# Degrees by a search in the sorted targets; all edge chunks scored behind the node projection

## Chip, cores and metric

The kernel runs on one core of one Trainium2 chip. The metric is the device time of one execution in microseconds (us): the median of three runs before was 3279.69 us (3274.05 to 3285.43). Engines: PE is TensorE (PEld its weight loads), DVE is VectorE, ACT is ScalarE, POOL is GpSimd, SP is SyncE; SPq and POOLq are the queues on which SyncE and GpSimd issue transfers.

## The reference, cut to what matters

Two rounds of a graph layer and a mixture-of-experts layer over N = 6250 nodes of D = 256 features and E = 100000 edges; `dst` is sorted. The change lies in the first stage of the first graph layer, on normed node rows:

```python
ft = (feat @ W_fc).reshape(N, H, D)               # H = 8 heads of 32
eh = jnp.einsum('nhd,hd->nh', ft, attn_h)
et = jnp.einsum('nhd,hd->nh', ft, attn_t)
fe = (edge_attr @ W_e).reshape(-1, H, D)          # 64 numbers an edge
ee = jnp.einsum('ehd,hd->eh', fe, attn_e)
e = leaky_relu(eh[src] + ee + et[dst])
... # softmax of e over the edges of each dst, then the weighted sum of ft[src]
```

Later stages also need the in-degree of every node (a mean over its edges) and the rank of every node among those that have edges.

## The kernel before

The program is a row of phases: `front` (L282 to L840), `attend` (L843 on: softmax and sums of the first graph layer), the gated experts, `sum_segments`, `mean_route` and `expert_tiles`. A phase ends with a barrier of all engines. Every order of work in `front` is written out by hand, one in-order list for each engine, with semaphores between them. `front` has these strands:

- **Node projection.** 50 columns of 125 nodes, two columns a group, so NGR = 25 groups. SyncE loads x in ten pieces (`load_x`, L400). VectorE takes statistics (`stats`, L694) and norms two columns (`norm`, L711). TensorE turns them (`turn`, L544: 4 transposes) and multiplies by the weights, extended by attn_h and attn_t (`project`, L553: 8 matmuls into two PSUM banks of which there is one set, so group g+1 waits until ScalarE has emptied group g). ScalarE copies the turned tile (`copy_turned`, L635) and empties the banks (`rows`, L641), whose two row buffers SyncE stores to the DRAM table `ft_rows` (`store`, L415). `rows(g)` waits for the store of group g-2.
- **Edge scores.** 49 chunks of 16 x 128 edges (NCH = 49), half a megabyte each, in four load buffers (`load`, L404: it waits until the chunk four before it is turned). TensorE turns a chunk (`turn_edges`, L517: 8 transposes), ScalarE copies it (`copy_edges`, L616), TensorE multiplies it by the folded edge weights (`score`, L528: 16 matmuls), ScalarE keeps the scores in the tile V (`keep`, L624). Chunks 0 to 24 run inside the 25 projection groups, chunks 25 to 48 behind them. `keep(0)` waits until the zeroes for `et_at_starts`, which SyncE stores from V, have landed (L442).
- **Degrees.** VectorE splits every dst into two digits (L722 to L728) and writes one-hots of both for each of the 49 chunks (`onehots`, L685), two chunks a group; TensorE counts them by 784 small matmuls into one bank (`count`, L537). Behind the last group VectorE turns the counts into degrees, prefix sums, first edges (FIRSTI) and ranks (L772 to L798).
- **GpSimd.** When the table of et is stored, it gathers one tile (L497), then scatters et to the first edge of each node by 50 indirect transfers (L503), which need FIRSTI, then gathers the first 64 of attend's 784 tiles of `ft_rows` (L511). The phase ends when all strands have ended. In attend GpSimd gathers the other 720 tiles (L975).
- **Ranks of edges.** VectorE marks where an edge has the dst of the one before it (CONTB, CONT) and scans these to ranks (L801 to L809). SyncE stores and reloads them in other layouts through DRAM, one transfer waiting for another (L454 to L476); the last of these is CONTU, a 1568 KB load that repeats its source eight times. No edge chunk is loaded while SyncE works through this list from L463 to L476. TensorE turns the ranks at one place among the chunks (`late`, L602 to L611).
- **The end.** SyncE loads the scattered et back into F (L481) once the scatters have landed, three chunks ahead of the last load. VectorE fills the gaps by 8 scans (L835), adds F to V in 7 parts (L840), and SyncE stores each part (L488) for attend.

Of the kernel before, what the change touches and what calls it, by code (L numbers as in the profile page):

```python
# [18 lines left out]
bf16 = mybir.dt.bfloat16  # L19
i32 = mybir.dt.int32  # L20
# [5 lines left out]
P = 125  # L26
# [255 lines left out]
def front(nc, sb, ps, sem, sems, x, src, dst, edge_attr, W_fc, attn_h, attn_t, W_e, attn_e, GX, a_in, ident, iota, below,  # L282
# [20 lines left out]
    with ExitStack() as s:  # L303
# [3 lines left out]
        ZB = sb(s, "ZB", [128, 128], bf16)  # L307
# [12 lines left out]
        HS = 4  # L320
        FB = F[:, :].bitcast(bf16)
        hotA = [FB[:, k * C * P:(k + 1) * C * P].rearrange("p (c a) -> p c a", a=P) for k in range(HS)]
        hotB = [FB[:, HS * C * P + k * C * NT:HS * C * P + (k + 1) * C * NT].rearrange("p (c b) -> p c b", b=NT)
                for k in range(HS)]
        QI = sb(s, "QI", [QB, NQ, EP], i32)
        QF = sb(s, "QF", [QB, NQ, EP])
        DA = sb(s, "DA", [EP, ES])
# [10 lines left out]
        DT = XNB[0:NT, NQ * EP:NQ * EP + P]  # L338
        CONTQ = QI[:, :, :].bitcast(bf16)[:, :, 0:EP]
        INC = sb(s, "INC", [P, 2, NT])  # L340
        NEQ = sb(s, "NEQ", [P, NT])
        UN = sb(s, "UN", [P, NT])
        TOT = sb(s, "TOT", [P, 2])
# [8 lines left out]
        BASEF = DA[0:1, :]  # L352
# [12 lines left out]
        w_ready, vb_ready, zb_ready = sem("w_ext_ready"), sem("vb_ready"), sem("zb_ready")  # L365
# [5 lines left out]
        hot, hot_used, counted = sem("hot"), sem("hot_used"), sem("degrees_counted")  # L371
        dt_ready, deg_ready, tot, pre, first_ready = (sem("degrees_copied"), sem("degrees_T"), sem("node_totals"),
                                                      sem("node_prefix"), sem("firsts_ready"))
# [14 lines left out]
        with nc.Block() as block:  # L388
            @block.sync
            def _(sp):  # L390
# [80 lines left out]
                sp.wait_ge(dt_ready, 1)  # L471
# [44 lines left out]
            def _(pe):  # L516
# [2079 lines left out]
```

## Time and profile before

| What | us |
|---|---|
| median of 3 runs | 3279.69 |
| the profiled execution: its own time / its span | 3277.21 / 3275.7 |
| front, up to the first instruction of attend | 401.2 |
| PE, DVE, POOL busy in the span | 2385.6, 1885.0, 1795.3 |

The trace is one execution. A window row gives its stretch and length, then the busy time (and number of instructions) of PE, PEld, DVE, ACT and POOL, then the granted TensorE clock as a share of full speed, the busy share of the 16 DMA engines, and GB/s. A timeline row gives start, duration, engine, line, operation, the tile written and read, the number of instructions merged, and in brackets the idle time before and what ended it; a row of merged ones shows their common stretch. A grouped line gives the number of instructions, their busy time and mean ns, and the idle time before them.

### The profile page before, as it was taken

The page shows a single profiled execution, that of the slowest core. Times are in us where ns is not written, and L with a number is a line of the kernel's source. Part 1 is how long each engine was busy: PE and PEld are TensorE (multiplying, and loading weights), DVE is VectorE, ACT ScalarE, POOL GpSimd, SP SyncE. Part 2 cuts the span into 40 slices and gives each one's busy share as a digit, 9 for nine tenths or more (in the row PEclk, how much of TensorE's full clock was granted, in tenths as well). Part 3 has the DMA queues.
Part 4 walks back from the last instruction along what each step waited for, and adds up shares of the span by engine and source line. Part 5 has one row for each costly group of instructions (what it writes and reads, how often), then busy time and mean ns, then how long its engine had stood idle before and what let it go on. Part 6 is the DMA issues. An engine that isn't in the chain of part 4 may idle for free. (4 is left out here: it accounts for less than half of the span.)

```text
span 3275.7 us, 49346 instructions
## 1 busy us (share of the span) xinstructions
PE 2385.6 (73%) x12682; PEld 1986.9 (61%) x12682; DVE 1885.0 (58%) x5767; ACT 1315.9 (40%) x4659; POOL 1795.3 (55%) x1886
## 2 busy tenths in 40 slices
PE   5995366667666665657899698888888888746088
PEld 4884256666666565446677576666666666635077
DVE  7981388888889887657455433333333333366245
ACT  2332255555555544523445333333333333355033
POOL 0007777777777777041000677777777777250645
PEclk9998778887888877778999656656565566757589
DMA  7336644444444445460000333333333333321342
GB/s 209 100 109 149 201 110 112 113 112 112 112 111 114 112 112 153 139 185 26 23 16 19 113 106 105 107 105 106 105 106 105 106 105 106 113 62 34 97 139 86
DMA packets 264113, 348.42 MB, mean 106 GB/s; under 512 B 153632, under 2 KB 193686, under 8 KB 262331
## 3 DMA queue, kind: packets, MB, share of 16 engines
q0 software_dynamic: 87936, 235.05, 25.3%
q1 hardware_dynamic: 175908, 110.32, 13.1%
q8 instruction: 103, 1.69, 0.2%
q14 instruction: 166, 1.36, 0.1%
HBM read 288.25 MB, written 61.20 MB: 107 GB/s over the span
## 5 line engine op out<-in xcount | busy, mean ns | idle before, releaser
L1384 POOL DMA_INDIRECT Gb<-normed_rows,SRCT x784 | 741.3, 946 | 519.6 <-SPq L1376 281.0
L1405 PE MATMUL pAb<-HOTb,Gb 128*128 128x128 f32 x3136 | 845.5, 426 | 149.4 <-DMA Gb<-normed_rows,SRCT 117.5
L1405 PEld LDWEIGHTS pAb<-HOTb,Gb 128*128 128x128 f32 x3136 | 659.6, 297 | 335.4 <-DMA Gb<-normed_rows,SRCT 274.7
L1445 DVE TENSOR_TENSOR ACC<-ACC,pAb 128x256 f32 x784 | 330.8, 422 | 641.8 <-PE pAb L1405 569.1
L975 POOL DMA_INDIRECT GX<-ft_rows,SRCT x432 | 413.3, 957 | 131.8 <-issue 128.6
L1064 ACT ACTIVATE ACC<-apA 128x254 f32 x784 | 300.4, 383 | 413.5 <-PE apA L1137 339.4
L1137 PE MATMUL apA<-AHOT,GX 128*128 128x129 f32 x1920 | 306.2, 330 | 81.1 <-DVE GX L1286 80.8
L1137 PEld LDWEIGHTS apA<-AHOT,GX 128*128 128x128 f32 x1920 | 292.2, 243 | 98.8 <-DVE GX L1286 98.6
L1424 ACT ACTIVATE HOTb<-OFFb 128x1024 f32<-128x1024 f32 x98 | 103.6, 1057 | 604.8 <-PE pAb L1405 604.7
L975 POOL DMA_INDIRECT G<-ft_rows,SRCT x288 | 273.8, 951 | 87.6 <-issue 87.1
L1420 ACT ACTIVATE OFFb<-iota,NRELb 128x128 f32<-128x128 f32 x784 | 239.6, 388 | 6.7
L1137 PE MATMUL apA<-AHOT,G 128*128 128x129 f32 x1216 | 192.3, 327 | 52.1 <-DVE G L1286 50.0
L1137 PEld LDWEIGHTS apA<-AHOT,G 128*128 128x128 f32 x1216 | 182.2, 239 | 64.4 <-DVE G L1286 62.1
L1286 DVE TENSOR_TENSOR GX<-GX,apV 128x1024 f32<-128x1024 f32 x120 | 143.1, 1193 | 0.0
L1614 POOL DMA_INDIRECT Y<-sums_by_rank,RANKI x50 | 48.4, 967 | 170.0 <-POOLq L152 80.8
L1065 ACT ACTIVATE FL<-apA 128x4 f32<-128x4 f32 x784 | 135.0, 172 | 0.0
L533 PE MATMUL pS<-VB,eT 128*128 128x128 f32 x784 | 105.2, 290 | 39.9 <-ACT V L628 22.8
L497 POOL DMA_INDIRECT C<-et_rows,DXI x1 | 2.6, 2577 | 233.7 <-DMA et_rows<-ETS 233.7
L533 PEld LDWEIGHTS pS<-VB,eT 128*128 128x128 f32 x784 | 96.3, 201 | 47.8 <-ACT eT L622 46.1
L2454 POOL DMA_INDIRECT out_dram<-sO,sID x80 | 77.8, 972 | 77.6 <-issue 40.9
L1186 DVE TENSOR_TENSOR AHOT<-apL,RELT 128x1024 f32<-128x1024 f32 x98 | 118.7, 1211 | 0.0
L1941 PE MATMUL fpM<-fxT,ffn_E 128*128 128x250 f32 x400 | 100.3, 405 | 25.0 <-ACT h L1869 25.0
(381 smaller groups left out, 4182.4 us busy)
## 6 DMA issues: line engine op xcount, KB each, us to landing
ebuf<-in_edge_attr_dram SPq DMA_DIRECT2D x49, 448.0 KB
Gb<-normed_rows,SRCT POOLq DMA_INDIRECT x784, 2.7
rows_by_expert<-ffn_PADT SPq DMA_DIRECT2D x1, 10360.0 KB, 42.3
sT<-rows_by_expert SPq DMA_DIRECT2D x80, 129.5 KB, 2.1
GX<-ft_rows,SRCT POOLq DMA_INDIRECT x480
sums_by_rank<-rrowa SPq DMA_DIRECT2D x49, 128.0 KB, 1.7
sums_by_rank<-rrowb SPq DMA_DIRECT2D x49, 128.0 KB, 1.7
GX<-in_x_dram SPq DMA_DIRECT2D x11, 560.0 KB
```

Of the source, the lines that this page charges most:

```text
L533: last = nc.tensor.matmul(pS[:, m * 2 * H0:m * 2 * H0 + 128], eT[c % 2][:, m * EP:(m + 1) * EP], VB[:, :], start=True, stop=True)
L975: pool.indirect_dma_start(G[c % GS][:, m, :], None, FT[:, :], bass.IndirectOffsetOnAxis(ap=SRCT[:, t:t + 1], axis=0)).then_inc(g_in[c % GS ...
L1064: nc.scalar.activation(acc[:, :, ds(r + 1, EP - 1)], sums[:, :, 1:EP], ACT.Copy)
L1065: nc.scalar.activation(FL[:, :, f:n + 1:n - f], sums[:, :, 0:HW:EP], ACT.Copy).then_inc(pfree[b], 1)
L1137: last = nc.tensor.matmul(pA[b][:, f * HW:(f + 1) * HW], G[c % GS][:, m, f * 128:(f + 1) * 128], HOT[c % 2][:, m, :], start=True, stop=True)
L1186: nc.vector.tensor_tensor(HOT[c % 2][:, h * HT:(h + 1) * HT, 0:EP], pL[0:EP, 256:256 + EP].unsqueeze(1).to_broadcast([EP, HT, EP]), RELT[: ...
L1286: nc.vector.tensor_tensor(v, v, pV[0:EP, 0:128].rearrange("p (h m) -> p h m", m=UT)[:, :, m:m + WB].rearrange("p h m -> p m h").unsqueeze( ...
L1384: pool.indirect_dma_start(G[g % R][m][:, :], None, TABLE[:, :], bass.IndirectOffsetOnAxis(ap=SRCT[:, t:t + 1], axis=0)).then_inc(g_in[g % ...
L1405: last = nc.tensor.matmul(pA[b][:, o:o + EP], G[k][m][:, c * 128:(c + 1) * 128], HOT[k % 2][:, m, :], start=True, stop=True)
L1420: nc.scalar.activation(OFF[k2][:, m, :], iota[0:EP, 0:EP], ACT.Abs, bias=NREL[k2][:, m:m + 1])
L1424: nc.scalar.activation(HOT[k2][:, :, :], OFF[k2][:, :, :], ACT.Relu, bias=1.0, scale=-1.0).then_inc(hot[k2], 1)
L1445: last = nc.vector.tensor_tensor(acc[:, :, ds(b, EP)], acc[:, :, ds(b, EP)], pA[q][:, o:o + KD * EP].rearrange("p (c r) -> p c r", c=KD), ...
```

## The change

- The digits, `onehots` and `count` go, with their zero matmuls and the transpose of the counts. In place of them: SyncE loads dst once more in another layout (DVI: 125 partitions of 25 x 32 sorted targets; SNI: the first target of the next partition). GpSimd makes two tables of node numbers. VectorE makes, in four batches of 12 or 13 columns, a one-hot of the partition that holds each node's first edge (`segment_hits`, 13 x 125 numbers in each of two instructions); TensorE fetches that partition's 25 word starts by 51 matmuls (`segments`, at groups 1 to 4); VectorE counts those below the node (`segment_rows`) and so knows the 32-word row. GpSimd gathers these rows by NV = 51 indirect transfers, ahead of everything it did before; VectorE counts inside them (`first_edges`) and gets first edges and, by differences, degrees. FIRSTI no longer needs the prefix matmul on TensorE.
- All 49 chunks are turned and scored behind the projection. Inside the projection SyncE issues no edge load beyond the first four.
- The small matmuls for ranks sit at chunks 12 and 13, the turn of ranks at chunk 24. The SyncE list of rank transfers begins behind the load of chunk 16.
- F is loaded behind the last edge load (it waits for `rq_ready` too, since F's memory now also holds BASEF), instead of three chunks ahead of it.

```diff
+        NV = NT + 1
+        SB = 13
+        SW = [min(SB, NV - b * SB) for b in range((NV + SB - 1) // SB)]
+        BW = 32
+        BK = E // BW // P
+        HITS = SB * P
+        NODE = F[0:P, 0:HITS]
+        OH = [F[0:P, (1 + k) * HITS:(2 + k) * HITS] for k in range(2)]
+        WORDS = F[:, HITS:HITS + NV * BW].bitcast(i32)
+        WORDF = F[0:P, HITS + NV * BW:HITS + 2 * NV * BW]
+        LT = F[0:P, 3 * HITS:3 * HITS + SB * BK]
+        DVI = F[0:P, 3 * HITS + SB * BK:3 * HITS + SB * BK + BK * BW].bitcast(i32)
...
+                ds32 = dst.rearrange("(p j) -> p j", j=BK * BW)
+                for a in PARTS:
+                    sp.dma_start(DVI[a, :], ds32[a, :]).then_inc(dv_in, 16)
+                sp.dma_start(SNI[0:P - 1, :], ds32[1:P, 0:1], allow_slow_non_contiguous=True).then_inc(dv_in, 16)
...
                 for g in range(NGR):
-                    if g > 0:
-                        load(g - 1 + ER)
                     store(g)
                 sp.dma_start(ETD.rearrange("(p i) h -> p (i h)", i=NT), ETS[0:P, :]).then_inc(etd_out, 16)
-                n = NGR - 1 + ER
-                load(n)
+                n = 4 * ER
+                for c in range(ER, n + 1):
+                    load(c)
...
-                for c in range(n + 3, NCH - 3):
+                for c in range(n + 3, NCH):
                     load(c)
+                sp.wait_ge(rq_ready, 1)
                 sp.wait_ge(st, 16 * NT)
                 sp.dma_start(F[:, :], STARTD.rearrange("(p j) h -> p (j h)", j=ES)).then_inc(f_in, 16)
-                for c in range(NCH - 3, NCH):
-                    load(c)
...
+                pool.wait_ge(rows_ready, 1)
+                dw = dst.rearrange("(r k) -> r k", k=BW)
+                for i in range(NV):
+                    pool.indirect_dma_start(WORDS[:, i * BW:(i + 1) * BW], None, dw,
+                                            bass.IndirectOffsetOnAxis(ap=ROWI[:, i:i + 1], axis=0)).then_inc(words_in, 16)
...
-                def count(c):
-                    pe.wait_ge(hot, c + 1)
-                    for m in range(C):
-                        last = nc.tensor.matmul(pH[0:NT, 0:P], hotB[c % HS][:, m, :], hotA[c % HS][:, m, :],
-                                                start=False, stop=False, skip_group_check=True)
-                    last.then_inc(hot_used, 1)
+                def segments(b):
+                    pe.wait_ge(oh_ready, b + 1)
+                    if b:
+                        pe.wait_ge(seg_read, b)
+                    for i in range(SW[b]):
+                        o = i * (BK + 1)
+                        last = nc.tensor.matmul(pH[0:P, o:o + 128], OH[b % 2][:, i * P:(i + 1) * P], SEG[:, :], start=True, stop=True)
+                    last.then_inc(seg_found, 1)
...
-                    turn_edges(g)
-                    count(2 * g)
+                    if 1 <= g <= len(SW):
+                        segments(g - 1)
                     if g + 1 < NGR:
                         turn(g + 1)
-                    if 2 * g + 1 < NCH:
-                        count(2 * g + 1)
-                    score(g)
                     project(g)
-                nc.tensor.matmul(pH[0:NT, 0:P], ZB[:, 0:NT], ZB[:, 0:P], start=False, stop=True,
-                                 skip_group_check=True).then_inc(counted, 1)
-                turn_edges(NGR)
-                pe.wait_ge(dt_ready, 1)
-                nc.tensor.transpose(pQ[0:P, 0:NT], DT[:, :], ident[0:NT, 0:NT]).then_inc(deg_ready, 1)
-                score(NGR)
-                turn_edges(NGR + 1)
-                pe.wait_ge(tot, 1)
-                for n in range(2):
-                    last = nc.tensor.matmul(pQ[0:P, 64 + n:65 + n], below[0:P, 0:P], TOT[:, n:n + 1], start=True, stop=True)
-                last.then_inc(pre, 1)
-                score(NGR + 1)
-                pe.wait_ge(rtot, 1)
-                nc.tensor.matmul(pT[:, 0:1], below[:, :], TOTR[:, :], start=True, stop=True).then_inc(rpre, 1)
...
-                    copy_edges(g)
                     if g + 1 < NGR:
                         copy_turned(g + 1)
-                    keep(g)
                     rows(g)
                     if g + 3 < NGR and chunk_of(g + 3) > chunk_of(g + 2):
                         root(chunk_of(g + 3))
-                copy_edges(NGR)
-                for c in range(NGR, NCH):
+                copy_edges(0)
+                for c in range(NCH):
...
+                def segment_hits(b):
+                    if b >= 2:
+                        dve.wait_ge(seg_found, b - 1)
+                    w = SW[b] * P
+                    nc.vector.tensor_scalar(OH[b % 2][:, 0:w], NODE[:, 0:w], SNX[:, b:b + 1], None, ALU.is_le)
+                    dve.drain()
+                    nc.vector.scalar_tensor_tensor(OH[b % 2][:, 0:w], NODE[:, 0:w], SX[:, b:b + 1], OH[b % 2][:, 0:w], ALU.is_gt,
+                                                   ALU.mult).then_inc(oh_ready, 1)
...
+                    v = pH[0:P, 0:w * (BK + 1)].rearrange("p (i k) -> p i k", k=BK + 1)
+                    lt = LT[:, 0:w * BK].rearrange("p (i k) -> p i k", k=BK)
+                    nc.vector.tensor_tensor(lt, v[:, :, 0:BK], NODEV[:, a].unsqueeze(2).to_broadcast([P, w, BK]), ALU.is_lt)
+                    nc.vector.tensor_copy(ROWF[:, a], v[:, :, BK]).then_inc(seg_read, 1)
+                    dve.drain()
+                    nc.vector.tensor_reduce(LESS[:, a], lt, AX.X, ALU.add)
...
+                def first_edges():
+                    dve.wait_ge(words_in, 16 * NV)
+                    nc.vector.tensor_copy(WORDF, WORDS[0:P, :])
+                    dve.drain()
+                    v = WORDF.rearrange("p (i k) -> p i k", k=BW)
+                    nc.vector.tensor_tensor(v, v, NODEV[:, :].unsqueeze(2).to_broadcast([P, NV, BW]), ALU.is_lt)
+                    dve.drain()
+                    nc.vector.tensor_reduce(LESS[:, :], v, AX.X, ALU.add)
+                    dve.drain()
+                    nc.vector.scalar_tensor_tensor(ROWF[:, :], ROWF[:, :], float(BW), LESS[:, :], ALU.mult, ALU.add)
+                    dve.drain()
+                    nc.vector.tensor_tensor(DEG[:, :], ROWF[:, 1:NV], ROWF[:, 0:NT], ALU.subtract)
...
-                    for c in range(2 * g + 2, min(2 * g + 4, NCH)):
-                        onehots(c)
+                    if 1 <= g <= len(SW):
+                        segment_rows(g - 1)
+                        if g + 1 < len(SW):
+                            segment_hits(g + 1)
...
+                nc.vector.tensor_tensor(FIRSTI[0:P, :], ROWF[:, 0:NT], UN[:, :], ALU.add).then_inc(first_ready, 1)
+                dve.wait_ge(f_ready, NGR)
+                nc.vector.tensor_tensor(CONT[:, :], DX[:, 1:ES + 1], DX[:, 0:ES], ALU.is_equal)
                 dve.wait_ge(pre, 1)
```

## Rows read from the trace of the kernel before

**Rows 1.** Busy time by stretch: the projection, the edge stage, the start.

```profile
54.00:234.00 180.00, 170.96 (x1547) 149.40 (x1546) 158.26 (x218) 62.04 (x191) 0.00 (x0) 0.98 0.37 104
295.00:360.00 65.00, 48.09 (x398) 44.15 (x397) 24.09 (x25) 20.09 (x48) 50.38 (x49) 1.00 0.79 230
16.00:56.00 40.00, 21.01 (x153) 18.37 (x154) 38.42 (x64) 5.54 (x18) 0.00 (x0) 0.87 0.99 293
```

**Rows 2.** Busy time in a stretch of attend; grouped lines of GpSimd in attend.

```profile
600.00:800.00 200.00, 137.80 (x837) 124.77 (x836) 176.23 (x611) 106.34 (x554) 151.56 (x160) 0.83 0.46 112
L975 POOL DMA_INDIRECT GX<-ft_rows,SRCT x432 | 413.3, 957 | 131.8 <-issue 128.6 <-PE apA L1137 3.3
```

**Rows 3.** Timeline of GpSimd: start us, duration us, what (later timelines alike).

```profile
244.79 1.21 POOL L503 DMA_INDIRECT et_at_starts<-ETS,FIRSTI  x1 [0.31 <-issue]
308.88 1.00 POOL L511 DMA_INDIRECT GX<-ft_rows,SRCT  x1 [0.30 <-issue]
393.99 0.94 POOL L511 DMA_INDIRECT G<-ft_rows,SRCT  x1 [0.30 <-issue]
401.17 0.10 POOL L935 MEMSET HSEL<- 128x8 f32 x1 [6.25 <-POOLq L152]
```

**Rows 4.** Timeline of TensorE, chunks 25, 47 and 48.

```profile
234.99 1.09 PE L524 MATMUL pE<-ident,ebuf 128*128 128x128 f32 x8
353.32 1.04 PE L524 MATMUL pE<-ident,ebuf 128*128 128x128 f32 x8
357.28 1.04 PE L524 MATMUL pE<-ident,ebuf 128*128 128x128 f32 x8
359.38 2.02 PE L533 MATMUL pS<-VB,eT 128*128 128x128 f32 x16 [1.06 <-ACT V L628]
```

**Rows 5.** Timeline of SyncE and VectorE at the front's end.

```profile
331.57 0.35 SPq L481 DMA_DIRECT2D F<-et_at_starts  x1
345.36 14.05 DVE L835 TENSOR_TENSOR_SCAN F<-xnT,C,F 128x784 f32<-128x784 f32 x8 [30.10 <-DMA F<-et_at_starts]
359.49 7.12 DVE L840 TENSOR_TENSOR V<-V,F 128x896 f32<-128x896 f32 x7
360.60 6.91 SPq L488 DMA_DIRECT2D score_parts<-V  x7
```

**Rows 6.** Timeline of SyncE and TensorE around the longest wait.

```profile
245.16 0.34 SPq L458 DMA_DIRECT2D edge_rank<-DB  x1
260.96 0.65 SPq L476 DMA_DIRECT2D CONTU<-goes_on_by_tile  x1
261.66 0.45 SPq L408 DMA_DIRECT2D ebuf<-in_edge_attr_dram  x1
284.77 1.97 PE L524 MATMUL pE<-ident,ebuf 128*128 128x128 f32 x8 [24.66 <-DMA ebuf<-in_edge_attr_dram]
291.24 1.92 PE L524 MATMUL pE<-ident,ebuf 128*128 128x128 f32 x8
```

**Rows 7.** Timeline of one projection group, TensorE and SyncE.

```profile
139.76 2.00 PE L560 MATMUL pF<-Wext,xnT 128*125 128x272 f32 x8
143.59 0.65 PE L549 MATMUL pT<-ident,xn 125*128 125x125 f32 x4
142.63 0.76 SPq L418 DMA_DIRECT2D ft_rows<-row  x2
```

**Rows 8.** Timeline of ScalarE and TensorE, first groups.

```profile
46.87 0.28 ACT L628 ACTIVATE V<-pS 128x128 f32<-128x128 f32 x1 [12.35 <-DMA sums_by_rank<-V]
52.46 3.06 PE L560 MATMUL pF<-Wext,xnT 128*125 128x272 f32 x8
```

**Rows 9.** Grouped lines of VectorE in the projection.

```profile
L689 DVE TENSOR_TENSOR F<-iota,DA 128x2000 bf16<-128x2000 f32 x41 | 91.6, 2235 | 0.0
L716 DVE TENSOR_SCALAR xn<-GX,MEAN,RSTD 125x256 f32<-125x256 f32 x40 | 14.7, 409 | 0.6
L279 DVE BATCH_NORM_STATS2 ST<-GX 125x6 f32<-125x256 f32 x40 | 13.8, 413 | 0.0
```

More of the change, by code:

```diff
@@ L318, in front @@
         eT = [sb(s, f"eT{k}", [128, C // 2 * EP]) for k in range(2)]
[L320 to L324, printed above, removed]
+        NV = NT + 1
[10 more added lines that the diff above has]
+        DVI = F[0:P, 3 * HITS + SB * BK:3 * HITS + SB * BK + BK * BW].bitcast(i32)
+        SNI = sb(s, "SNI", [P, 1], i32)
+        SX = sb(s, "SX", [P, len(SW)])
+        SNX = sb(s, "SNX", [P, len(SW)])
+        SEG = sb(s, "SEG", [P, 128])
+        NODEV = sb(s, "NODEV", [P, NV])
+        ROWF = sb(s, "ROWF", [P, NV])
+        LESS = sb(s, "LESS", [P, NV])
+        ROWI = sb(s, "ROWI", [128, NV], i32)
         QI = sb(s, "QI", [QB, NQ, EP], i32)
         QF = sb(s, "QF", [QB, NQ, EP])
-        DA = sb(s, "DA", [EP, ES])
         DB = sb(s, "DB", [EP, ES])
@@ L370, in front @@
         sc_ready, v_ready = sem("edge_scores"), sem("edge_scores_kept")
-        hot, hot_used, counted = sem("hot"), sem("hot_used"), sem("degrees_counted")
-        dt_ready, deg_ready, tot, pre, first_ready = (sem("degrees_copied"), sem("degrees_T"), sem("node_totals"),
-                                                      sem("node_prefix"), sem("firsts_ready"))
+        dv_in, node_set = sem("dst_segments_in"), sem("node_numbers_set")
+        oh_ready, seg_found, seg_read = sem("segment_onehots"), sem("segments_found"), sem("segments_read")
+        rows_ready, words_in = sem("dst_rows_known"), sem.gather("dst_rows_in")[0]
+        tot, pre, first_ready = sem("node_totals"), sem("node_prefix"), sem("firsts_ready")
         etd_out, cont_ready, cont_out, cq_in = sem("et_out"), sem("cont_ready"), sem("cont_out"), sem("cont_by_tile")
@@ L562, in project @@
                     last.then_inc(f_ready, 1)
-                pe.wait_ge(zb_ready, 1)
-                nc.tensor.matmul(pH[0:NT, 0:P], ZB[:, 0:NT], ZB[:, 0:P], start=True, stop=False, skip_group_check=True)
                 pe.wait_ge(qf_ready, 1)
@@ L663, in _ @@
                         root(chunk_of(g + 3))
-                copy_edges(NGR)
-                for c in range(NGR, NCH):
+                copy_edges(0)
+                for c in range(NCH):
                     if c + 1 < NCH:
@@ L683, in _, with segment_bounds @@
                 nc.vector.memset(UN[:, :], 1.0)
-                def onehots(c):
-                    if c >= HS:
-                        dve.wait_ge(hot_used, c - HS + 1)
-                    for to, a, w in ((hotA, DA, P), (hotB, DB, NT)):
-                        last = nc.vector.tensor_tensor(to[c % HS], iota[:, 0:w].unsqueeze(1).to_broadcast([EP, C, w]),
-                                                       a[:, c * C:(c + 1) * C].unsqueeze(2).to_broadcast([EP, C, w]),
-                                                       ALU.is_equal)
-                    last.then_inc(hot, 1)
+                def segment_bounds():
+                    dve.wait_ge(dv_in, 48)
+                    dve.wait_ge(node_set, 5)
+                    nc.vector.tensor_copy(SEG[:, 0:BK], DVI[:, 0:BK * BW:BW])
+                    nc.vector.tensor_copy(SX[:, 0:1], DVI[:, 0:1])
+                    nc.vector.tensor_copy(SNX[:, 0:1], SNI[:, :])
+                    dve.drain()
+                    nc.vector.memset(SX[0:1, 0:1], -1.0)
+                    dve.drain()
+                    for b in range(1, len(SW)):
+                        for v in (SX, SNX):
+                            nc.vector.tensor_scalar(v[:, b:b + 1], v[:, 0:1], float(b * SB), None, ALU.subtract)
+                    dve.drain()
@@ new lines, in segment_rows @@
+                def segment_rows(b):
+                    dve.wait_ge(seg_found, b + 1)
+                    w, a = SW[b], slice(b * SB, b * SB + SW[b])
+                    v = pH[0:P, 0:w * (BK + 1)].rearrange("p (i k) -> p i k", k=BK + 1)
[5 more added lines that the diff above has]
+                    dve.drain()
+                    nc.vector.tensor_scalar(LESS[:, a], LESS[:, a], 1.0, 0.0, ALU.subtract, ALU.max)
+                    dve.drain()
+                    nc.vector.tensor_tensor(ROWF[:, a], ROWF[:, a], LESS[:, a], ALU.add)
+                    dve.drain()
+                    if b == len(SW) - 1:
+                        nc.vector.tensor_copy(ROWI[0:P, :], ROWF[:, :]).then_inc(rows_ready, 1)
@@ L758, in _ @@
                     nc.vector.tensor_copy(SRCT[:, n * 4 * QB:n * 4 * QB + w], of[0:EP, 0:w]).then_inc(src_ready, 1)
+                segment_bounds()
+                segment_hits(0)
                 norm(1)
                 stats(1)
+                segment_hits(1)
                 for g in range(NGR):
```

71 lines of the change are left out of this document (34 added, 37 removed).

## Prediction

> **What bounds the kernel now.** I read the busy time by stretch first, then the timeline of each engine through `front`, then attend. In the 180 us of the projection TensorE is busy for 171 and VectorE for 158, at a granted clock of 0.98 [rows 1]: both in-order lists are nearly full, while GpSimd does nothing at all. The projection ends where chunk 25 starts, at 235.0 [rows 4]. Only then does GpSimd begin: 50 scatters from 244.8, row gathers from 308.9, the last issued at 394.0; attend starts at 401.2 [rows 3]. The edge chain is done earlier: chunk 48 is turned at 357.3 [rows 4], the parts are stored by 367.5 [rows 5]. So the end of `front` is set by GpSimd, with some 27 us to spare for the edge chain, and GpSimd is late because FIRSTI and the table of et come at the projection's end.
>
> What is won before attend is won in full: in attend GpSimd issues one gather each 1.25 us without a rest (160 in 200 us, waiting for TensorE 3.3 us in 432) [rows 2]. It has the same 64 tiles in hand when attend starts, before and after.
>
> **The projection.** Out of each group go one edge chunk and two chunks of counting. What stays is project, 2.00 us for 8 matmuls, then ScalarE's emptying of the banks: the store is issued at 142.63, 0.87 after the matmuls' end at 141.76 [rows 7]. The next project needs those banks; with an estimated 0.1 for the hand-over a group takes 2.97 us. The turn (0.65) [rows 7] fits under the emptying. VectorE's share, two norms at 0.41, two columns of statistics at 0.41 and small ones, is under 2 us [rows 9]. Now a group takes 180/24.5 = 7.3.
>
> The start does not shrink so. From 16 to 56 us the DMA engines are 99% busy [rows 1]: x, four edge chunks and the zeroes. ScalarE waited there until 46.9 for the zeroes [rows 8]; that wait leaves the projection with `keep(0)`, but `rows(2)` needs the store of group 0, which is queued behind x. So I put `rows(2)` at about 54, and group 3 runs at half clock as the matmuls at 52.46 did (3.06 for 8) [rows 8]: done at 57.6. Then 21 groups at 2.97 = 62.4, and some 3 for the batch of segments in group 4 (13 matmuls like those of a score, 2.02 for 16 [rows 4], so 1.6) and for roots: the projection ends at **123** instead of 235. Bounds: 118, and 146 if all 22 groups run at half clock (1.06 more each).
>
> **The search.** Removed from VectorE: 49 times 2.2 and 1.0 us. Added: per batch two instructions of 1625 numbers; at 1.12 ns a number, the rate of the one-hot (2235 ns for 2000) [rows 9], 3.6 us at most, and about 2 for `segment_rows`. Four batches, 22 us, fall into the first 58 us, where x is awaited anyway. The three further dst loads on SyncE delay x at the start by 1 to 3 us, and GpSimd's two tables delay the zeroes by about as much; the zeroes are awaited by no group any more, and the loads are in the 118 to 123. The fourth batch is read at about 61. GpSimd's 51 gathers are nowhere in this trace; the nearest rows are the scatters, (308.88 - 244.79)/50 = 1.28 us each with the small gather between left out [rows 3]: 65 us, so 127. Low bound 1.25 as in attend; high bound 2.0. They lie in time that was idle. `first_edges` and FIRSTI: two passes of 1632 numbers at 1.12 ns, one cheaper and ten small ones, 8 us, after an estimated 2 for landing: 137. Then 64 us of scatters, to 201, and 64 row gathers, which took 86 [rows 3]: 287. At the high bound of the gathers, 324. GpSimd is no longer last. TensorE wants the totals first at chunk 12, 123 + 48 = 171, 34 us later than they come.
>
> **The edge chain** now decides. Undisturbed, a chunk takes 357.28 - 353.32 = 3.96 us [rows 4], at a granted clock of 1.00 although DMA is 79% busy [rows 1]. So 48 chunks to the start of chunk 48: 190 us. Four buffers are full at the start, so nothing is late at once.
>
> Disturbed: the rank transfers. In this trace the store of ranks goes out at 245.2, CONTU at 261.0, the next edge load at 261.7, and that load has landed only at 284.8: 23.1 us; TensorE waited 24.7 us. It restarts at half clock, so that the two turns at 284.77 and 291.24 are 6.5 apart, 3 us lost in all [rows 6]. After the change the ranks are stored 2.4 us after chunk 13 starts, CONTU 15.8 later, load 19 0.8 later still: 19.0 after chunk 13. Chunk 19 would start 23.8 after chunk 13. If the landing takes 23.1 again, TensorE waits 18 us. But the row gathers begin near 201, while CONTU (issued at 123 + 51.5 + 18.2 = 193) is still on its way: 128 rows of 1056 bytes each 1.25 us, 108 GB/s. I add 3 us and take **21**. Bounds: 0, if what made it slow was something else, and 45, if the landing doubles. Ranks are turned among the chunks as now (2 us).
>
> Chunk 48 starts at 123 + 190 + 21 + 3 + 2 = **339**, 18 us earlier than now.
>
> **The tail** is longer than that chain's was. F is loaded when chunk 44 has been turned, 14 us ahead of chunk 48's start, not 26: issued at 325.5. It took 345.36 - 331.57 = 13.8 us beside gathers and edge loads [rows 5]; the gathers are over by then, so 12 (bounds 9 and 14): 337.5. Scans 14.05, adds 7.12 [rows 5]: 358.7. Last store issued 1 later; with 2 for its landing and GpSimd's 6.25 before the barrier opens [rows 3], attend starts at **368** instead of 401.2.
>
> The sum: 33 us less. On the profiled execution, 3277.2 - 33 = 3244; its time is 2.5 below the median, so I forecast 3246.
>
> On the 23 us of landing, one rule speaks against the change. The Trainium skill (DMA: Bandwidth & Descriptors, Issuing engines are not separate DMA queues) has all issuers' transfers interleave on the same 16 engines. No row shows CONTU beside row gathers. If they shared for 15 of the 23 us, 1.6 MB more at the rate of the landing (1568 KB and one load of 512 KB in 23.1 us, 92 GB/s) would be 17 us, and the sum 3260; my 3 us go by the time at which the gathers start.
>
> **The rivals.**
> 1. *The wait at CONTU disappears or shrinks*, since 12 chunks earlier in the chain other transfers stand around it. For it: 1568 KB in 23 us is far below the 293 GB/s of the start [rows 1, 6]. Against it: the same list of transfers, with scatters beside it as before. Without waits and cold restart, 24 us less: 3222. Chance 0.12.
> 2. *Less is won*: the projection at half clock (23 us) or a wait of over 35 us; 3262 to 3272. For it: TensorE idles 0.3 of every 2.97 us and the first matmuls after a pause ran at half speed [rows 8]. Against it: 1.06 us gaps in 3.96 left the clock at 1.00 [rows 1, 4]. Chance 0.16.
> 3. *Slower*: TensorE stays at its lower clock of 1.2 GHz in the edge stage. A chunk then costs about 6.4 instead of 3.96 (the 6.5 between the turns after the wait [rows 6]). 33/2.44 = 14 cold chunks undo the gain; all 49 would give 3246 + 120 = 3366, half of them 3306. For it: only 77% of a chunk is matmul time. Against it: 65 us at 1.00 in just this loop [rows 1]. Chance 0.10. The Trainium skill (TensorE: Matmul & The Clock Gate, What's actually happening) says that the default state is throttled and activity releases it; the cold restart [rows 6] agrees.
> 4. *GpSimd still ends last*, so that the change only moves work: its chain would have to end 75 us later than 287, each new gather costing 2.7 us, or `rows_ready` come at 136. Then 3280. Chance 0.04.
>
> The forecast keeps 0.58. A measurement of this kernel can tell 0.3%, 10 us, from no change; faster means under 3270. That holds for the forecast, rival 1 and most of rival 2: 0.81; same 0.08; slower 0.11. The range: from rival 1 with a start at 118 (3217) to rival 2 with both of its causes in part (3276).
>
> **What would show it.** Right: chunk 0 turned near 123; granted clock near 1 in projection and edge stage; 51 gathers at 1.28 us from about 61; one wait of 15 to 30 us at chunk 19; the last gather of `front` near 285; F's scans end behind the last score; attend from 368. Wrong: a group of the projection over 4 us; a wait for the totals at chunk 12; several waits for edge loads; attend's gathers no longer at 1.25 us.

## The result, and the profile after

| | before | after |
|---|---|---|
| median, us (range) | 3277.07 (3274.05 to 3285.43), 4 runs | 3245.34 (3242.41 to 3248.20), 4 runs |
| ratio, 95% interval | | 0.990 (0.988 to 0.992) |
| the profiled execution: time / span | 3277.21 / 3275.7 | 3244.61 / 3242.9 |
| attend starts | 401.2 | 369.7 |

The change makes the kernel 32 us faster, 1.0%, with an interval clear of 1; 3246 was forecast, in a range of 3217 to 3276. Attend starts 31.5 us earlier, nearly the whole of the gain. In two later batches of experiments every kernel was slower, the one before included (3782 and 3789 us); they have a section of their own and are compared with nothing else.

Busy time by stretch of the changed kernel (columns as in [rows 1]):

```profile
54.00:234.00 180.00, 122.15 (x772) 104.41 (x772) 51.51 (x175) 56.10 (x182) 114.43 (x118) 0.90 0.54 131
295.00:360.00 65.00, 39.75 (x329) 36.81 (x328) 15.73 (x10) 17.59 (x43) 0.00 (x0) 0.95 0.42 133
203.00:256.00 53.00, 26.44 (x188) 23.69 (x186) 8.37 (x28) 9.80 (x23) 40.21 (x43) 0.77 0.94 210
```

In the first stretch VectorE does a third of its former work and GpSimd, which had done nothing, is busy for 114 us. In the second GpSimd is already done. The third is the one to remember: TensorE is busy half the time, while the DMA engines are 94% busy (their busy share; they move 210 GB/s in it).

Timeline of the changed kernel, GpSimd (first row: the end of the word gathers; last row: the start of attend):

```profile
133.30 0.94 POOL L522 DMA_INDIRECT F<-in_dst_dram,ROWI  x1 [0.30 <-issue]
139.53 0.94 POOL L526 DMA_INDIRECT C<-et_rows,DXI  x1 [5.29 <-DMA et_rows<-ETS]
149.36 1.01 POOL L532 DMA_INDIRECT et_at_starts<-ETS,FIRSTI  x1 [8.89 <-DVE FIRSTI L843]
292.96 0.95 POOL L540 DMA_INDIRECT G<-ft_rows,SRCT  x1 [0.30 <-issue]
369.69 0.10 POOL L986 MEMSET HSEL<- 128x8 f32 x1 [75.78 <-POOLq L152]
```

The last row gather goes out at 293 instead of 394 [rows 3], and GpSimd then idles for 76 us. It no longer decides anything here.

ScalarE and TensorE of the same kernel: the first wait for a row buffer, a batch of segments, the matmuls of the last projection group, chunks 0, 18, 19 and 20:

```profile
59.57 0.39 ACT L665 ACTIVATE row<-pF 125x264 f32<-125x264 f32 x1 [15.30 <-DMA ft_rows<-row]
```
```profile
64.28 3.82 PE L572 MATMUL pH<-SEG,F 125*125 125x128 f32 x24
...
129.53 2.07 PE L591 MATMUL pF<-Wext,xnT 128*125 128x272 f32 x8 [0.99 <-ACT ETS L666]
131.44 1.04 PE L553 MATMUL pE<-ident,ebuf 128*128 128x128 f32 x8
...
202.55 1.04 PE L553 MATMUL pE<-ident,ebuf 128*128 128x128 f32 x8
225.62 1.97 PE L553 MATMUL pE<-ident,ebuf 128*128 128x128 f32 x8 [18.96 <-DMA ebuf<-in_edge_attr_dram]
232.08 1.81 PE L553 MATMUL pE<-ident,ebuf 128*128 128x128 f32 x8
```

SyncE around the rank list, and SyncE and VectorE at the end of `front`:

```profile
185.05 0.35 SPq L474 DMA_DIRECT2D edge_rank<-DB  x1
200.87 0.64 SPq L491 DMA_DIRECT2D CONTU<-goes_on_by_tile  x1
201.55 0.45 SPq L421 DMA_DIRECT2D ebuf<-in_edge_attr_dram  x1
...
331.67 0.36 SPq L497 DMA_DIRECT2D F<-et_at_starts  x1
359.45 6.33 SPq L502 DMA_DIRECT2D score_parts<-V  x7
```
```profile
344.20 14.05 DVE L886 TENSOR_TENSOR_SCAN F<-xnT,C,F 128x784 f32<-128x784 f32 x8 [84.24 <-DMA F<-et_at_starts]
358.33 7.10 DVE L891 TENSOR_TENSOR V<-V,F 128x896 f32<-128x896 f32 x7
```

These rows answer to [rows 4 to 6]: the same wait at the load behind CONTU, 19 us, and the same tail of load, scans, adds and stores, now on the path.

### The profile page after: what moved, and what is told of

Read it like the earlier page. It is cut to its first block and busy times, and to the rows that moved or that the text cites. A ratio compares the mean times of both kernels' runs of the same rounds, so it can differ in the third digit from the quotient of the medians.

```text
span 3242.9 us, 47998 instructions
## 1 busy us (share of the span) xinstructions
PE 2347.0 (72%) x11995; PEld 1955.5 (60%) x11995; DVE 1756.4 (54%) x5705; ACT 1314.1 (41%) x4659; POOL 1838.9 (57%) x1942
## 5 line engine op out<-in xcount | busy, mean ns | idle before, releaser
L1026 POOL DMA_INDIRECT GX<-ft_rows,SRCT x432 | 412.6, 955 | 131.4 <-issue 129.6
L1188 PEld LDWEIGHTS apA<-AHOT,G 128*128 128x128 f32 x1216 | 189.2, 247 | 59.2 <-DVE G L1337 56.8
L2253 POOL DMA_INDIRECT rows_by_expert<-PAY,POSI x50 | 49.6, 992 | 123.4 <-DVE POSI L2444 108.5
```

The costliest lines, as they stand in the source:

```text
L1026: pool.indirect_dma_start(G[c % GS][:, m, :], None, FT[:, :], bass.IndirectOffsetOnAxis(ap=SRCT[:, t:t + 1], axis=0)).then_inc(g_in[c % GS ...
L1188: last = nc.tensor.matmul(pA[b][:, f * HW:(f + 1) * HW], G[c % GS][:, m, f * 128:(f + 1) * 128], HOT[c % 2][:, m, :], start=True, stop=True)
```

## Experiments

Two questions. Which part of the change won the 32 us? And what is the edge chain, which now decides, really waiting for?

### The two parts, each alone

**The search alone**: chunks 0 to 24 run inside the projection groups again, the rank list is where it was before.

```diff
 # load, turn_edges, copy_edges, score and keep, once in each group g
+                    turn_edges(g)
+                    score(g)
-                early, late = 3 * ER, 6 * ER
-                for c in range(NCH):
+                early, late = NGR + 1, NGR + 10
+                for c in range(NGR, NCH):
```

> Theory A (the search pays, moving the chunks gives part of it back): with 25 chunks beside the projection again, a group takes about 5.7 us instead of 3.06 and 7.3, the projection ends near 188, chunk 48 starts near 305 instead of 345, and GpSimd, which starts its scatters near 198, becomes the last again with its last row gather near 345. Attend starts near 351 instead of 369.7, and the kernel takes about 3227 us, faster than the changed kernel. Theory B (both parts are needed, since the chunks crowd the projection on TensorE): 3250 us or more.

Measured: 3237.75 us (3236.97 to 3239.78), ratio to before 0.989 (0.987 to 0.990). That is 7.6 us *under* the full change, or 5.0 when each is taken against the before of its own batch (3277.07 there, 3274.49 here); the two ratios' intervals overlap, so the times alone do not show a difference, but attend starts 6.1 us earlier too. TensorE and GpSimd of this kernel:

```profile
98.26 1.04 PE L554 MATMUL pE<-ident,ebuf 128*128 128x128 f32 x8
104.20 1.04 PE L554 MATMUL pE<-ident,ebuf 128*128 128x128 f32 x8
...
245.91 1.97 PE L554 MATMUL pE<-ident,ebuf 128*128 128x128 f32 x8 [24.71 <-DMA ebuf<-in_edge_attr_dram]
```
```profile
205.29 1.11 POOL L527 DMA_INDIRECT C<-et_rows,DXI  x1 [62.60 <-DMA et_rows<-ETS]
363.54 0.10 POOL L991 MEMSET HSEL<- 128x8 f32 x1 [6.04 <-POOLq L152]
```

A group with a chunk in it now takes 5.8 us instead of 7.3, and GpSimd idles only 6 us before attend: here its chain ends last, as before the change. What starts it is no longer FIRSTI, which needs only the word gathers, but the table of et at the end of the projection (the wait of 62.60). Theory A had the direction, but 10 us too much gain; theory B is out.

**The move alone**: one-hots and counting as before, all 49 chunks behind the projection.

> Theory A and the sum of the prediction: the one-hots keep VectorE at some 8 us a group, so the projection still ends at 215 to 235, all 49 chunks come behind it, and attend starts at 455 to 475: 3330 to 3350 us, slower than both kernels. A rival, that the chunks were what filled a group and not the counting: the projection ends before 160 and the kernel is at 3280 or below.

Measured: one run, 3322.66 us, 48 above the 3274.5 of before, 7 under the range of theory A. Chunk 0 is turned at 221.7, only 13 us earlier than the projection's end in [rows 4], since the groups still carry their counting, and the whole edge chain comes behind it:

```profile
448.45 0.10 POOL L929 MEMSET HSEL<- 128x8 f32 x1 [73.10 <-POOLq L152]
```

What follows: against the before of their batches, the search alone gives -37, the move alone +48, both -32. The move costs 48 without the search; with it, it wins nothing that was measured and more likely costs 5 to 8. All of the gain is the search's.

### The wait behind the rank list

CONTU reads 16 partitions of a DRAM table and writes them eight times, by a leading dimension of 8 with zero stride. **CONTU in eight transfers** writes the same bytes:

```diff
-                sp.dma_start(CONTU[:, 0:NCH * EP], CONTP.unsqueeze(0).to_broadcast([H0, UT, NCH * EP])).then_inc(cu_in, 16)
+                for h in range(H0):
+                    sp.dma_start(CONTU[h * UT:(h + 1) * UT, 0:NCH * EP], CONTP[:, :]).then_inc(cu_in, 16)
```

> CONTU is loaded by eight transfers of 16 partitions instead of one whose outermost dimension is the repeat of eight. Theory C (the repeat in front confines the transfer to eight engines, and the edge loads behind it wait for these): the next edge load lands 10 to 14 us after its issue instead of 24, TensorE waits under 9 us instead of 19, and the kernel takes 3231 to 3236 us. Rival (the bytes or the small scatters beside them are slow, whatever the shape): landing stays over 20 us and the time at 3243 to 3248.

Measured: one run, 3234.84 us, attend at 359.00.

```profile
199.11 4.29 SPq L492 DMA_DIRECT2D CONTU<-goes_on_by_tile  x8
203.45 0.43 SPq L421 DMA_DIRECT2D ebuf<-in_edge_attr_dram  x1
```
```profile
215.04 1.97 PE L554 MATMUL pE<-ident,ebuf 128*128 128x128 f32 x8 [11.50 <-DMA ebuf<-in_edge_attr_dram]
```

The edge load behind the list lands 11.6 us after its issue instead of 24.1; issuing costs SyncE 3.7 more. TensorE waits 11.5 instead of 19.0, a gain of 7.5; the other 3.2 of the 10.7 by which attend comes earlier are the projection's (chunk 0 at 128.3 instead of 131.4), which the edit does not touch; the time is 10.5 us under the change, or 7.9 with each taken against the before of its batch. The Trainium skill (DMA: Bandwidth & Descriptors, Rules for kernel authors) says that an outermost dimension of size c under 16, a leading broadcast for instance, keeps a transfer to at most c of the 16 engines. The halved landing agrees. The engines' busy share does not show the other eight idle: it is 0.97 from 203 to 226 in the changed kernel and 0.97 from 199 to 216 here. So the shape of the transfer is shown to be the cause, and the way in which it acts is not. The wait stayed above the 9 us I had given as its ceiling.

### The tail

**F loaded earlier**, behind the load of chunk 32:

```diff
                 for c in range(n + 3, NCH):
                     load(c)
+                    if c == 32:
+                        sp.wait_ge(rq_ready, 1)
+                        sp.wait_ge(st, 16 * NT)
+                        sp.dma_start(F[:, :], ...).then_inc(f_in, 16)
```

> F is loaded behind the load of chunk 32 instead of behind that of chunk 48. Theory D (the tail behind the last chunk is scans and adds that need not stand there): the scans are over before chunk 48, six of seven adds as well, attend starts near 355 instead of 369.7, and the kernel takes about 3231 us. Rival (3.1 MB beside row gathers and edge loads make TensorE wait for edge loads, and the scans slow the gathers): a new wait of 8 us or more at a chunk between 33 and 40, 3238 us or more.

Measured: one run, 3231.30 us.

```profile
282.22 14.06 DVE L886 TENSOR_TENSOR_SCAN F<-xnT,C,F 128x784 f32<-128x784 f32 x8 [21.78 <-DMA F<-et_at_starts]
```
```profile
281.70 0.94 POOL L540 DMA_INDIRECT G<-ft_rows,SRCT  x1 [0.30 <-issue]
282.95 1.88 POOL L540 DMA_INDIRECT G<-ft_rows,SRCT  x1 [0.30 <-issue]
285.13 1.44 POOL L540 DMA_INDIRECT G<-ft_rows,SRCT  x1 [0.30 <-issue]
...
354.93 0.10 POOL L986 MEMSET HSEL<- 128x8 f32 x1 [56.66 <-POOLq L152]
```

Attend starts 14.8 us earlier; the time is 14.0 us under the change, or 11.5 with each taken against the before of its batch. No edge chunk behind F waited (the wait at chunk 19 stayed, 19.2 us): from 234 on the edge loads had gone out one each 3.955 us again, as buffers came free, and the four buffers covered the transfer. The price is small and lies on an idle path: beside VectorE's scans a gather of GpSimd takes 1.44 us instead of 0.94 (one 1.88).

### All waits at once, and what came back

If each wait stood wholly on the chain, taking three away should give their sum. This kernel keeps all chunks behind the projection, moves the zeroes and the first four edge loads behind the store of group 3, spreads the eight pieces of CONTU over the loads of chunks 19 to 26, and loads F behind chunk 32.

```diff
                     store(g)
+                    if g == 3:
+                        ...  # the zeroes' two stores
+                        for c in range(ER):
+                            load(c)
...
                 for c in range(n + 3, NCH):
                     load(c)
+                    h = c - (n + 3)
+                    if h < H0:
+                        sp.dma_start(CONTU[h * UT:(h + 1) * UT, ...], CONTP[:, :]).then_inc(cu_in, 16)
+                    if c == 32:
+                        ...  # F
```

> The kernel with all waits taken away, once more: in the two earlier batches the kernel before took 3782 and 3789 us where it had taken 3275, and in the traces of the changed kernels TensorE and ScalarE stood nearly still while GpSimd issued the 51 word gathers (PE busy 24.9 of the 66 us from 56 to 122, against 52.1 in the changed kernel), so they say nothing of the waits. If the kernel before takes 3270 to 3285 again, theory A (the chain of edge chunks decides, and each wait stood wholly on it) gives projection end 121 to 124, TensorE's wait for the edge load of chunk 19 under 3 us, attend at 322 to 330 and 3198 to 3206 us, a ratio of 0.977 to before. Theory B (the chains share the gain: the row gathers of GpSimd end last) gives attend at 330 to 345 with GpSimd idle under 10 us before it, and 3207 to 3222 us. If the kernel before takes over 3700 again, a ratio over 1.005 as before is expected, and no theory is told apart.

Measured: 3232.77 us (3226.65 to 3235.18), before 3276.03 there, ratio 0.986 (0.984 to 0.987); attend at 353.14, GpSimd idle 68.8 before it. All three theories miss. TensorE of this kernel, chunks 19 to 29, and the two behind F:

```profile
203.71 1.09 PE L557 MATMUL pE<-ident,ebuf 128*128 128x128 f32 x8
207.72 1.04 PE L557 MATMUL pE<-ident,ebuf 128*128 128x128 f32 x8
213.00 1.09 PE L557 MATMUL pE<-ident,ebuf 128*128 128x128 f32 x8 [1.16 <-DMA ebuf<-in_edge_attr_dram]
219.85 1.09 PE L557 MATMUL pE<-ident,ebuf 128*128 128x128 f32 x8 [2.68 <-DMA ebuf<-in_edge_attr_dram]
...
251.09 1.39 PE L557 MATMUL pE<-ident,ebuf 128*128 128x128 f32 x8
255.40 1.04 PE L557 MATMUL pE<-ident,ebuf 128*128 128x128 f32 x8
...
281.89 1.97 PE L557 MATMUL pE<-ident,ebuf 128*128 128x128 f32 x8 [6.56 <-DMA ebuf<-in_edge_attr_dram]
```

The one long wait is gone, as asked. But the nine chunks from 203.71 to 255.40 take 51.7 us, where nine at 3.955 are 35.6: 16.1 us lost in sips. Of these 2 are the turn of ranks and 7.2 the waits for edge loads; over part of the rest TensorE ran at its lower clock (0.87 granted on the mean of the stretch below). Counted the same way, the kernel that issued the eight pieces in one burst took 44.3 us for the seven chunks from 199.42 to 243.72, instead of 27.7: 16.6 lost, again with 2 for the turn of ranks. Burst or spread, it is about 16 us. And F, which had cost nothing in the kernel before this one, cost a wait of 6.6 here. The stretches:

```profile
203.00:256.00 53.00, 36.48 (x243) 32.32 (x243) 10.21 (x20) 11.40 (x27) 40.03 (x43) 0.87 1.04 217
256.00:300.00 44.00, 28.04 (x206) 25.84 (x205) 19.16 (x13) 11.40 (x27) 22.20 (x21) 0.88 1.00 282
```

The DMA engines are at 1.04 and 1.00. I read from this that with the edge loads, the row gathers and the rank list together they are full, and that what is moved about within the stretch is paid all the same. The share alone does not prove it: at 1.04 they moved 217 GB/s, at 1.00 they moved 282. A second cause stands in every kernel here: SyncE issues no edge load while it works through the rank list. In the changed kernel load 19 could have gone when chunk 15 was turned, at 191.7, and went at 201.55, so 10 of the 15.8 us that four full buffers last were used up before CONTU was issued. No kernel tests what edge loads issued among the transfers of the list would bring.

The zeroes did the same on a small scale: the wait of 15.3 for a row buffer at `rows(2)` went, and one of 10.7 came at `rows(6)`, behind the zeroes. The projection ended at 128.5, 2.9 us earlier and not 8 to 10, and not even that is shown to be their doing, for in the kernel with CONTU in eight transfers, which changes nothing there, it ended at 128.3.

```profile
71.67 0.39 ACT L669 ACTIVATE row<-pF 125x264 f32<-125x264 f32 x1 [10.73 <-DMA ft_rows<-row]
```

### The work that belongs beside the projection

During the projection of the changed kernel the DMA engines are idle for most of the time (0.33 busy from 56 to 122). So a last kernel puts chunks 0 to 10 beside groups 12 to 22 again, the zeroes in seven pieces behind the stores of groups 2 to 8, loads 0 to 3 behind those of groups 8 to 11, CONTU in eight pieces at its old place, F behind chunk 36.

```diff
+                    if 12 < g <= 23:
+                        load(g - 1 - 12 + ER)
                     store(g)
+                    if 2 <= g < 9:
+                        zw = ES * H0 // 7
+                        sp.dma_start(STARTD...[:, (g - 2) * zw:(g - 1) * zw], V[:, (g - 2) * zw:(g - 1) * zw])...
+                    if 8 <= g < 8 + ER:
+                        load(g - 8)
...
+                    if 12 <= g < 23:
+                        turn_edges(g - 12)
                     if g + 1 < NGR:
                         turn(g + 1)
+                    if 12 <= g < 23:
+                        score(g - 12)
                     project(g)
```

> Search kept, chunks 0 to 10 turned and scored beside groups 12 to 22 of the projection and 38 behind it, the zeros in 7 pieces of 448 KB behind the stores of groups 2 to 8, the loads of chunks 0 to 3 behind those of groups 8 to 11, the rank list in 8 pieces at its old place, the node features for the last adds behind the load of chunk 36. Theory D (behind the projection the DMA engines are the limit, 1.04 busy from 203 to 256 in the run with all chunks behind, so that a transfer moved about there is paid for all the same, some 16 us for the rank list; beside the projection they are a third busy): work moved beside the projection is won. Projection end at 150 to 158 (128.5, + 11 x 2.7 for the chunks, less 0 to 8 for the zeros in pieces), then 38 x 3.955 = 150 and 16 for the rank list, and no wait for the node features: edge chain ends at 317 to 325, attend at 322 to 330 against 353.1, GpSimd idle some 10 to 20 us before it, time 3202 to 3210. Theory A' (every wait can be hidden, the DMA engines have room): the stall at the rank list is under 8, attend at 312 to 320, time under 3201. Theory E (GpSimd decides: the row gathers start as late as the projection ends and are slowed by what is moved beside them): GpSimd idles under 5 us before attend, attend at 335 or later, 3215 us or more.

Measured: **3197.09 us** (3191.82 to 3199.25, 5 runs), before 3279.26 (3269.46 to 3283.88), ratio 0.974 (0.973 to 0.976). TensorE at chunks 11 and 19, GpSimd at the end, and the stretches:

```profile
148.16 1.04 PE L561 MATMUL pE<-ident,ebuf 128*128 128x128 f32 x8
...
191.32 1.97 PE L561 MATMUL pE<-ident,ebuf 128*128 128x128 f32 x8 [11.37 <-DMA ebuf<-in_edge_attr_dram]
```
```profile
306.50 0.95 POOL L548 DMA_INDIRECT G<-ft_rows,SRCT  x1 [0.30 <-issue]
321.23 0.10 POOL L1002 MEMSET HSEL<- 128x8 f32 x1 [13.79 <-POOLq L152]
```
```profile
56.00:122.00 66.00, 57.05 (x361) 48.08 (x360) 28.02 (x115) 30.41 (x104) 48.50 (x51) 1.00 0.66 189
203.00:256.00 53.00, 39.45 (x311) 36.34 (x312) 9.52 (x16) 15.80 (x39) 40.20 (x43) 0.97 0.75 200
```

The time is 5 us under the range of theory D and would suit theory A'; the stall at the list, 11.4 and not under 8, speaks for D. The projection ended at 148.2, a little under my 150, and attend started at 321.2 instead of 322 to 330. GpSimd is now idle for 14 us before attend instead of 76. This version is 82 us under the kernel before and 48 under the change.

The kernel differs from the one with all waits taken away in several things at once, but its trace tells them apart. Of the 31.9 us by which attend starts earlier,

- 10.8 are there at group 11, ahead of any chunk (76.0 instead of 86.8): the zeroes in pieces, the first edge loads later, and no wait for a row buffer;
- 13.1 are the eleven chunks, which lengthen the projection by 2.8 us each and spare 3.955 each behind it;
- 9.6 are F, for which no chunk waited;
- 1.6 are lost at the rank list: from chunk 18 to 25 it took 45.0 us instead of 27.7, so the list costs what it cost before.

This shows that work moved beside the projection is won. That the DMA engines are the reason is not shown for the chunks: TensorE, too, waits for ScalarE in each of them, 0.56 us in a group and 1.06 in a chunk, and side by side the two can fill each other's gaps, whatever the DMA engines do. Nor is 0.75 against 1.04 a like comparison. CONTU now goes out at 174, outside that stretch, and around it, from 176 to 192, the share is as high as ever:

```profile
176.00:192.00 16.00, 3.57 (x27) 3.18 (x26) 3.86 (x16) 1.26 (x3) 12.09 (x13) 0.76 0.98 166
```

### Three kernels in two slower batches

The kernel with all waits taken away, the one with only the zeroes moved, and one with all waits taken away and chunks 0 to 10 beside groups 8 to 18 ran in two batches in which before took 3782 and 3789 us; the first of them was on the chip on which before had taken 3274. The second batch:

> The changed kernel, with one thing moved: the store of 3.2 MB of zeros (and the small one behind it) is issued behind the store of the node projection's group 3 instead of ahead of the first store. Theory A (the first store's rows stand behind the zeros in the DMA queues, which were 0.99 busy in that stretch): the wait of the first row statistics ends at 48 to 52 us instead of 59.6, the projection ends at 121 to 124 instead of 131.4, attend starts at 360 to 363 and the execution takes 3235 to 3238 us. Theory B (the loads of x and of the weights are what fills the queues): that wait ends within 2 us of 59.6, and the time stays at 3243 to 3246. Theory C (the zeros delay groups 3 to 6 instead): the first wait is shorter, but a new one of some 8 us stands on the row statistics of groups 4 to 7, and the projection ends at 129 to 132.

> As the one with all waits taken away, and chunks 0 to 10 are turned and scored beside groups 8 to 18 of the projection again, the other 38 behind it. Theory A (each chunk beside the projection takes 5.8 - 3.06 = 2.7 us more of the projection, in which GpSimd waits for the scatters' turn, and saves one chunk of 3.96 behind it, so 1.25 off the edge chain): projection end at 150 to 154, attend at 312 to 320, time 3188 to 3196, some 10 under the one with all waits taken away. Theory B (GpSimd decides from the start: the row gathers end later than the edge chain by more than it saved): attend at 325 or later, no gain over the other.

> The changed kernel with all edge chunks still behind the projection, and the waits of the stages around it taken away together: zeros and the loads of edge chunks 0 to 3 behind the store of group 3, the rank list in 8 pieces of 16 partitions spread one by one behind the loads of chunks 19 to 26, and the node features for the last adds loaded behind the load of chunk 32. Theory A (the chain of edge chunks decides, each of these waits stands wholly on it, and GpSimd stays ahead): projection end at 121 to 124, the wait of TensorE for the edge load of chunk 19 under 3 us instead of 19, attend at 322 to 330 instead of 369.7, time 3198 to 3206. Theory B (the gains overlap: the row gathers of GpSimd become the longer chain): GpSimd idles under 10 us before attend. Theory C (the list of ranks in pieces is late now): the segment searches wait for the rank list, chunks 19 to 26 each wait for their edge load, and attend starts at 340 or later.

Measured: 3867.16 (zeroes alone, one run), 3817.37 (with chunks 0 to 10 beside, ratio to before 1.007, 1.005 to 1.008) and 3824.93 (all waits away, 1.009, 1.007 to 1.011); the first batch gave 3858.91, 3814.81 and 3826.43. None of the times tells the theories apart. The zeroes alone have thus no time that can be compared; what is known of them comes from the kernels above. The stretch from 56 to 122 us, for the zeroes alone and for all waits away, shows where part of the time went:

```profile
56.00:122.00 66.00, 24.91 (x104) 18.40 (x102) 13.39 (x54) 8.66 (x32) 44.72 (x48) 0.66 0.27 85
```
```profile
56.00:122.00 66.00, 18.64 (x66) 12.91 (x64) 11.01 (x45) 7.25 (x27) 48.40 (x51) 0.64 0.33 89
```

While GpSimd issues its word gathers at the usual pace, TensorE, VectorE and ScalarE stand nearly still; the same kernel had 47.11 us of TensorE there when before took 3276. Once the gathers were out, the groups ran at 3.06 us again, and the projection ended at 175 instead of 128.5. The greater loss came behind it, beside the scatters and row gathers, which the kernel before has too. All waits away, from 182 to 330 us:

```profile
182.00:330.00 148.00, 19.68 (x114) 18.45 (x112) 0.00 (x0) 5.34 (x12) 110.17 (x115) 0.57 0.29 77
```

Chunk 6 was turned only at 300.7, the other 42 followed when GpSimd was done, and attend started at 521.6, not 353.1, with GpSimd idle for 194 us before it. The kernel before scores 25 of its 49 chunks ahead of its first scatter, and these kernels none or 11. So the moved chunks are a likelier reason than the search why they lost ground against before; no trace of the kernel before was taken in these batches, so this is not shown. The DMA engines were 0.29 busy in that stretch and were not what held TensorE up. Why every kernel was slower there, and through what the gathers held the others up, was not found.

## Why the prediction was right, point by point

- **What bounds the kernel**: right. GpSimd went from last to 76 us early, and attend's start fell by 31.5 us (33 forecast). In attend itself 160 gathers still take 200 us.
- **GpSimd's chain**: 51 gathers at 1.25 us (1.28 forecast), the last at 133.3 (127); they began at 70.3, not 61. VectorE could read them 6.8 us after the last one's end, not 2. FIRSTI at 148.3 (137), the last gather at 293.0 (287): the 64 row gathers took 80 us, not 86, since no scans ran beside them (see the end). Late by 6 in all, in time nobody waited for.
- **`rows(2)`**: mis-sized. "I put `rows(2)` at about 54"; it was 59.57. The store of group 0 stands not only behind x but behind the zeroes and four edge loads as well. I had put the zeroes down as "awaited by no group any more", and forgot that the store is. With both moved behind later stores, and the zeroes in pieces, no group waited. This is 5.6 of the 8.4 us by which the projection ended late.
- **The segments**: misread. I took 1.6 us for a batch of 13 small matmuls; a batch is 24 to 26 records, 3.0 us warm and 3.8 cold. With this, with group 3 at 3.96 us for its matmuls instead of 3.06, and with the groups at 3.06 us (2.97 forecast), the projection ended at 131.4, not 123, still in the bounds of 118 to 146.
- **The chunk**: 3.955 us at a granted clock of 1.00 (3.96). Rival 3, a cold TensorE for the whole stage, did not come; the clock fell only over waits (0.77 from 203 to 256).
- **The rank list**: 15.8 us from the ranks' store to CONTU, as forecast; then 24.1 to the landing (23.1 + 3 forecast), TensorE's wait 19.0 (21). The rule I weighed there, that all issuers share the 16 engines, would have made it 17 more in place of 3. It did not show in that landing, and could show little: the row gathers began at 214, not 201, when 11 of its 24 us were left.
- **The tail**: mis-sized the other way. F took 12.5 (12) and the scans 14.05, but attend opened 3.9 us after the last store's issue, 4.3 sooner than my 2 + 6.25. The 6.25 had stood behind a row gather [rows 3] and so held that gather's landing too.
- Three errors, +8.4 for the projection, -2 for the wait and -4.3 for the tail, came out at +2. That the sum hit 3245.3 within 1 us is partly luck.
- **Rival 4**, GpSimd last, did not come, and its price was worked out wrong: 75 us later than 287 would bring its end only level with the edge chain at 368. For the 3280 given there it had to be 107 us later, or 3.4 us a gather.
- **What I did not ask**: whether the second part was worth anything. My argument compared the change as a whole. That it would load all chunks in the fuller stretch could be read from [rows 1]: the DMA engines were 0.37 busy beside the projection and 0.79 behind it. It also put all 49 chunks, not 24, beside GpSimd's gathers, which cost dearly in the slower batches.

## What to carry to other kernels

Test the parts of a change one by one, even when the whole wins: here one part gave all and the other seems to have taken 5 to 8 us back. Before you move a transfer out of a wait's way, read the DMA share of the stretch: where it was near 1 here, spreading the transfer only spread the wait. What helped was a better shape of the transfer, full buffers in front of it, and moving whole pieces of work to a stretch in which those engines, and TensorE, had idle time. When two chains end a phase, trade between them until they end together.

## What was not expected of the hardware

- A load with a leading broadcast of 8 landed, with the load behind it, in 24.1 us; the same bytes in eight transfers of 16 partitions, in 11.6.
- Beside 14 us of scans on VectorE, GpSimd's gathers went from 0.94 to 1.44 us each, and came back to 0.94 when the scans ended. The Trainium skill (GPSIMD Engine Reference, 1. Specifications) says that GpSimd shares its interfaces to SBUF with VectorE and that they collide where a VectorE instruction has two inputs in SBUF; the scans read CONT and F there, and the trace agrees. The kernel before shows it as well, on the chain that ended last there: beside its scans and adds twelve gathers took 6.3 us more than twelve others.

```profile
348.27 1.44 POOL L511 DMA_INDIRECT GX<-ft_rows,SRCT  x1 [0.30 <-issue]
```

- In two batches the kernel before took 15% longer than in the others, once on the chip of the first four experiments and once on another. There the other engines nearly stopped while GpSimd issued gathers and scatters (TensorE busy for 18.6 of 66 us, against 47.1 in the same kernel elsewhere, and for 19.7 of the 148 us behind the projection), so that this kernel, 1.4% faster than before in one batch, was 0.9% slower in the other.
